# Short products as plain fp32 matmuls in a convolution and two-attention kernel on one core

## The reference

```python
# block 1
perceived = conv3x3_depthwise(x, w_perc) + b_perc        # 3 results for each channel
hid = gelu(w_up1 @ perceived + b_up1)                    # 256 channels
h = x + w_up2 @ hid + b_up2
q, k, v = split(h @ w_qkv.T + b_qkv)
scores = stack([(q * shifted(k, dy, dx)).sum(-1) for the 9 neighbours]) / sqrt(128)
h = h + sum(softmax(scores)[i] * shifted(v, i))
# block 2
xn = group_norm(h) * gamma + beta                        # 8 groups
q, k, v = xn @ Wq + bq, xn @ Wk + bk, xn @ Wv + bv
out = softmax(q @ k.T / sqrt(128)) @ v                   # 1024 x 1024
return xn + out @ Wp + bp
```

## Time and profile before

| | us |
|---|---|
| median of 3 runs | 1099.22 (1096.4 to 1099.63) |
| span of the profiled execution, first to last instruction | 1098.3 |
| PE busy | 1064.8 |
| PEld busy | 976.7 |
| DVE busy | 905.1 |
| ACT busy | 781.0 |
| POOL busy | 443.6 |

### The profile page before, as it was taken

One profiled execution on the slowest core, in us unless ns is written; L12 is line 12 of the kernel. 1 busy time (PEld: TensorE's weight loads), 2 busy tenths in 40 slices (PEclk: granted clock), 3 DMA queues, 4 the chain that ended last, 5 costly groups with the idle time before them and its releaser, 6 DMA issues.

```text
span 1098.3 us, 22684 instructions
## 1 busy us (share of the span) xinstructions
PE 1064.8 (97%) x7476; PEld 976.7 (89%) x7476; DVE 905.1 (82%) x1885; ACT 781.0 (71%) x1504; POOL 443.6 (40%) x399
## 2 busy tenths in 40 slices
PE   5988999999999999999999999999999999999997
PEld 5867989989899999999999999999999999998876
DVE  6957888788887888888788888878898888888874
ACT  2565686868677777767777776787777778677763
POOL 4634245361524527152452715335261533523130
PEclk9967999999999999999999999999999999999998
DMA  5101001020100102010010201001020100000000
GB/s 89 20 1 20 1 11 30 1 40 1 30 10 17 21 0 38 0 29 10 11 27 0 38 0 29 10 10 29 0 38 0 29 10 10 10 1 10 11 20 20
DMA packets 85496, 18.67 MB, mean 17 GB/s; under 512 B 67536, under 2 KB 85328, under 8 KB 85456
## 3 DMA queue, kind: packets, MB, share of 16 engines
q1 hardware_dynamic: 84608, 17.77, 8.7%
q10 hardware_dynamic: 848, 0.39, 0.2%
HBM read 9.76 MB, written 8.39 MB: 17 GB/s over the span
## 4 chain that ended last, share of the span: by engine, by line
PE 92%; DVE 4%; issue 2%; ACT 1%; POOL 1%; DMA 0%; ACTq 0%; DVEq 0%
PE work L476 20%; PE work L478 20%; PE work L477 20%; PE ps_t L636 10%; PE ps_s L476 5%; PE ps_s L477 5%; PE ps_s L478 5%; PE work L654 1%; PE work L562 1%; PE work L602 1%; PE work L571 1%; PE ps_t L664 1%; DVE et_lo L2006 1%; POOL g_lo L1519 1%; ACT et_hi L1104 0%
## 5 line engine op out<-in xcount | busy, mean ns | idle before, releaser
L1519 POOL TENSOR_TENSOR g_lo<-u,g_hi 128x512 fp32r<-128x512 f32 x60 | 78.2, 1304 | 349.4 <-ACT g_hi L1001 349.4
L1104 ACT ACTIVATE et_hi<-ps_t 128x1024 fp32r<-128x1024 f32 x128 | 131.1, 1024 | 66.4 <-PE ps_t L636 65.2
L2000 DVE TENSOR_REDUCE nm<-ps_s 128x1 f32<-128x1024 f32 x124 | 151.5, 1222 | 30.5 <-PE ps_s L478 28.9
L476 PE MATMUL work<-t_lo,wc_hi 128*128 128x256 f32 x576 | 166.8, 290 | 5.9 <-DVE wc_lo L1786 4.5
L2006 DVE TENSOR_TENSOR et_lo<-ps_t,et_hi 128x1024 fp32r<-128x1024 f32 x128 | 155.9, 1218 | 11.6 <-ACT et_hi L1104 8.9
L478 PE MATMUL work<-t_hi,wc_hi 128*128 128x256 f32 x576 | 162.7, 282 | 0.0
L477 PE MATMUL work<-t_hi,wc_lo 128*128 128x256 f32 x576 | 162.2, 282 | 0.0
L1094 ACT ACTIVATE e<-ps_s,nm 128x1024 f32<-128x1024 f32 x124 | 138.3, 1115 | 21.9 <-DVE nm L2000 19.8
L476 PE MATMUL work<-et_lo,vv_hi 128*128 128x256 f32 x512 | 147.5, 288 | 0.1
L478 PE MATMUL work<-et_hi,vv_hi 128*128 128x256 f32 x512 | 144.9, 283 | 0.0
L477 PE MATMUL work<-et_hi,vv_lo 128*128 128x256 f32 x512 | 144.5, 282 | 0.0
(11 more groups left out here) (213 smaller groups left out, 2965.0 us busy)
## 6 DMA issues: line engine op xcount, KB each, us to landing
x_in<-in_x SPq DMA_DIRECT2D x64, 128.0 KB, 3.4
out<-r_tok SPq DMA_DIRECT2D x32, 256.0 KB, 2.3
w_up_t<-in_L_conv_w_up SPq DMA_DIRECT2D x1, 384.0 KB, 4.3
y<-in_L_conv_w_qkv SPq DMA_DIRECT2D x1, 192.0 KB, 4.6
const<-in_const ACTq DMA_DIRECT2D x1, 166.0 KB, 5.6
y<-in_L_conv_w_up ACTq DMA_DIRECT2D x1, 128.0 KB, 5.5
const<-in_const ACTq DMA_DIRECT2D x1, 64.0 KB, 3.6
bv_row<-in_L_conv_b_qkv SPq DMA_DIRECT2D x1, 64.0 KB, 2.8
```

Of the source, the lines that this page charges most:

```text
L476: te.matmul(dst, wh, xl, start=first, stop=False)
L1104: act.activation(et_hi[:, :, (t % 4) * 128:(t % 4 + 1) * 128], ps_t[:, :].rearrange("p (k c) -> p k c", k=TILES), ACT.Copy) \
L1519: return pool.tensor_tensor(dst, full, hi, ALU.subtract)
L2000: dve.tensor_reduce(nm1[:, t:t + 1], score_tile(n, t)[:, :], AX.X, ALU.max, negate=True) \
```

## The change

Products with fewer than 256 moving columns lose their split operands: `v`, `local_scores`, `local_values` and `attended` become plain fp32 products. With that go `q_lo`, `kp_lo`, `v_hl`, `pt_lo`, `a_lo` and the instructions that made them, the matmul against zeros, and, because `attended` now takes the attended pixels as the stationary operand and so gives pixels on partitions, ACT's copy `a_t` and the transposes `final_t` as well. `v` reads `h` itself, so that it waits for `h_ready` and no longer for `h_lo_ready`. The transposed local weights get a buffer for each half image, and `halo_turn` writes straight into it. The bank of `pj` is now freed by DVE's `output`. All other calls keep their order on their engines.

```diff
-        kp_hi, kp_lo = (sb(f"kp_{p}", [128, HP, WP], F32R) for p in ("hi", "lo"))
-        v_full = sb("v_full", [128, 4, 128])
-        v_hl = sb("v_hl", [128, TILES, 2, 128], F32R)
+        q_c = sb("q_c", [128, PIX])
+        kp = sb("kp", [128, HP, WP])
+        v_pix = sb("v_pix", [128, TILES, 128])
...
-        pt_hi, pt_lo = (sb(f"pt_{p}", [128, 2 * W + 4 * WINDOW], F32R) for p in ("hi", "lo"))
+        pt_both = sb("pt", [128, 2, 2 * W + 4 * WINDOW])
+        pt = [pt_both[:, half] for half in range(2)]
...
-        FREED_BY = dict(conv=u_step, up2=h_ready, q=q_lo_ready, k=k_lo_ready, v=v_ready,
-                        at=pt_lo_ready, av=y_ready, gn=gn_step, qq=qq_lo_ready, kk=kk_lo_ready,
-                        vv=vv_lo_ready, pv=a_lo_ready, pj=a_t_ready, ft=o_ready, s0=e_ready, s1=e_ready)
+        FREED_BY = dict(conv=u_step, up2=h_ready, q=q_ready, k=k_ready, v=v_ready,
+                        at=pt_ready, av=y_ready, gn=gn_step, qq=qq_lo_ready, kk=kk_lo_ready,
+                        vv=vv_lo_ready, pv=a_ready, pj=o_ready, s0=e_ready, s1=e_ready)
...
             def v(n, half):
-                project_pixels("v", half, n, h_lo_ready, (w0_hi[:, 2], w0_lo[:, 2]), (h_hi, h_lo))
+                te.wait_ge(*h_ready.after(n, half))
+                te.wait_ge(*bank_free("v", half, n))
...
+                for t in range(4):
+                    pix = slice(half * HALF + t * 128, half * HALF + (t + 1) * 128)
+                    mm = te.matmul(bank("v", half, n)[:, t * 128:(t + 1) * 128], h[:, pix], wv0[:, :], start=True, stop=True)
+                mm.then_inc(pe["v"].handle, 1)
             def local_scores(n, j):
-                te.wait_ge(*q_lo_ready.after(n, j // 2))
-                te.wait_ge(*k_lo_ready.after(n, 1))
+                te.wait_ge(*q_ready.after(n, j // 2))
+                te.wait_ge(*k_ready.after(n, 1))
...
-                    qs = [x[:, t * 128:(t + 1) * 128] for x in (q_hi, q_lo)]
-                    ks = [x[:, 4 * t:4 * t + 6, :].rearrange("p r w -> p (r w)") for x in (kp_hi, kp_lo)]
-                    mm = mm3(dst, qs, ks)
+                    mm = te.matmul(dst, q_c[:, t * 128:(t + 1) * 128],
+                                   kp[:, 4 * t:4 * t + 6, :].rearrange("p r w -> p (r w)"), start=True, stop=True)
...
             def local_values(n, half):
-                te.wait_ge(*pt_lo_ready.after(n, 2 * half + 1))
-                te.wait_ge(*halo_lo_ready.after(n, half))
-                te.wait_ge(*v_lo_ready.after(n, 1))
+                te.wait_ge(*pt_ready.after(n, 2 * half + 1))
+                te.wait_ge(*halo_ready.after(n, 2 * half + 1))
+                te.wait_ge(*v_ready.after(n, 1))
...
-                te.matmul(dst[:, :].rearrange("p (r w) -> p r w", r=ROWS), w0_hi[:, 2],
-                          kp_hi[:, 0:1, 0:W].broadcast_to([128, ROWS, W]), start=True, stop=False)
                 for u in range(4):
                     t, before, behind = 4 * half + u, W if u else 0, W if u < 3 else 0
                     at = own_at(u)
-                    mm3(dst[:, u * 128 - before:(u + 1) * 128 + behind], (v_hl[:, t, 0, :], v_hl[:, t, 1, :]),
-                        [x[:, at - before:at + 128 + behind] for x in (pt_hi, pt_lo)], False, False)
+                    te.matmul(dst[:, u * 128 - before:(u + 1) * 128 + behind], v_pix[:, t, :],
+                              pt[half][:, at - before:at + 128 + behind], start=(u == 0), stop=False, skip_group_check=True)
...
             def attended(n, half):
-                te.wait_ge(*a_lo_ready.after(n, 2 * half + 1))
+                te.wait_ge(*a_ready.after(n, 2 * half + 1))
                 te.wait_ge(*bank_free("pj", half, n))
...
-                mm3(bank("pj", half, n)[:, :], (w1_hi[:, 2], w1_lo[:, 2]), (a_hi[:, :], a_lo[:, :])) \
-                    .then_inc(pe["pj"].handle, 1)
+                for t in range(4):
+                    pix = slice(t * 128, (t + 1) * 128)
+                    mm = te.matmul(bank("pj", half, n)[:, pix], a_c[:, pix], wv1[:, :], start=True, stop=True)
+                mm.then_inc(pe["pj"].handle, 1)
...
-            def final_t(n, half):
-                te.wait_ge(*a_t_ready.after(n, half))
-                te.wait_ge(*bank_free("ft", half, n))
-                for t in range(4):
-                    mm = te.transpose(bank("ft", half, n)[:, t * 128:(t + 1) * 128], a_t[:, t * 128:(t + 1) * 128], ident)
-                mm.then_inc(pe["ft"].handle, 1)
...
-            def halo_hi(n, half):
-                act.wait_ge(*halo_turned.after(n, 2 * half + 1))
-                act.wait_ge(*pe["av"].after(n, half - 1))
...
-            def v_lo_half(n, k):
-                pool.wait_ge(*v_hi_ready.after(n, k))
-                minus(v_hl[:, 4 * k:4 * k + 4, 1, :], v_full[:, :, :], v_hl[:, 4 * k:4 * k + 4, 0, :].bitcast(F32)) \
-                    .then_inc(v_lo_ready.handle, 1)
...
-                dve.wait_ge(*halo_lo_ready.after(n, j // 2 - 1))
-                dve.transpose(halo_t[0:W, two, :], pn[96:128, :, W + 128:WINDOW])
-                dve.transpose(halo_t[96:128, two, :], pn[0:W, :, 0:W]).then_inc(halo_turned.handle, 1)
...
+                dve.wait_ge(*pe["av"].after(n - 1, j // 2))
+                if is_first(n):
+                    dve.wait_ge(*cleared.after(0, 0))
+                dve.transpose(left_blocks(pt[j // 2])[:, two, :], pn[96:128, :, W + 128:WINDOW])
+                dve.transpose(right_blocks(pt[j // 2])[:, two, :], pn[0:W, :, 0:W]).then_inc(halo_ready.handle, 1)
...
-                dve.wait_ge(*pe["ft"].after(n, k))
+                dve.wait_ge(*pe["pj"].after(n, k))
```

More of the change, by code:

```diff
@@ L255, in conv_seq_kernel @@
         r_tok = sb("r_tok", [128, 4, 128])
-        a_at = region("a_mem", HALF)
-        a_hi, a_t = placed("a_hi", [128, HALF], a_at, F32R), placed("a_t", [128, HALF], a_at)
-        a_lo = sb("a_lo", [128, HALF], F32R)
+        a_c = sb("a_c", [128, HALF])
         bp_row = sb("bp_row", [128, 128])
@@ L575, in local_values @@
                     at = own_at(u)
-                    mm3(dst[:, u * 128 - before:(u + 1) * 128 + behind], (v_hl[:, t, 0, :], v_hl[:, t, 1, :]),
-                        [x[:, at - before:at + 128 + behind] for x in (pt_hi, pt_lo)], False, False)
+                    te.matmul(dst[:, u * 128 - before:(u + 1) * 128 + behind], v_pix[:, t, :],
+                              pt[half][:, at - before:at + 128 + behind], start=(u == 0), stop=False, skip_group_check=True)
                 t, rows, at = (4, 3 * 128 + 96, own_at(4) - W) if half == 0 else (3, 0, own_at(-1) + 128)
-                mm3(dst[:, rows:rows + W], (v_hl[:, t, 0, :], v_hl[:, t, 1, :]),
-                    [x[:, at:at + W] for x in (pt_hi, pt_lo)], False, True) \
-                    .then_inc(pe["av"].handle, 1)
+                te.matmul(dst[:, rows:rows + W], v_pix[:, t, :], pt[half][:, at:at + W],
+                          start=False, stop=True, skip_group_check=True).then_inc(pe["av"].handle, 1)
             def group_moments(n):
@@ L761, in fill_program @@
                 scores(0, 6)
-                final_t(0, 0)
                 probs_t(0, 5)
@@ L784, in fill_program @@
                 vv(1, 1)
-                final_t(0, 1)
             def turn_program(it):
@@ L826, in turn_program @@
                 v(c, 0)
-                final_t(a, 0)
                 scores(a, 7)
@@ L842, in turn_program @@
                 vv(b, 1)
-                final_t(a, 1)
             def drain_program():
@@ L880, in drain_program @@
                 k(B - 1, 0)
-                final_t(B - 3, 0)
                 up2(B - 1, 1)
@@ L911, in drain_program @@
                 probs_t(B - 2, 2)
-                final_t(B - 3, 1)
                 values(B - 2, 0)
@@ L926, in drain_program @@
                 group_moments(B - 1)
-                final_t(B - 2, 0)
                 values(B - 2, 2)
@@ L943, in drain_program @@
                 scores(B - 1, 3)
-                final_t(B - 2, 1)
                 vv(B - 1, 0)
@@ L958, in drain_program @@
                 probs_t(B - 1, 6)
-                final_t(B - 1, 0)
                 probs_t(B - 1, 7)
@@ L1014, in q_hi_half, with k_half @@
                     act.wait_ge(*scaled.after(0, 0))
[L1015 to L1018 removed]
+                act.activation(q_c[:, k * HALF:(k + 1) * HALF], bank("q", k, n)[:, :], ACT.Identity, bias=bq0_s) \
+                   .then_inc(q_ready.handle, 1)
+            def k_half(n, k):
                 act.wait_ge(*pe["k"].after(n, k))
@@ L1106, in et_hi_tile, with a_part @@
                    .then_inc(et_hi_ready.handle, 1)
-            def a_hi_part(n, j):
+            def a_part(n, j):
                 act.wait_ge(*pe["pv"].after(n, j))
-                act.wait_ge(*pe["ft"].after(n, j // 2 - 1))
-                act.activation(a_hi[:, (j % 2) * 256:(j % 2 + 1) * 256], bank("pv", j, n)[:, 0:256], ACT.Copy) \
-                   .then_inc(a_hi_ready.handle, 1)
-            def a_t_half(n, half):
```

(18 more changed lines are left out.)

349 lines of the change are left out of this document (94 added, 255 removed), and 20 rows, old and new, of tables (BANK_PLAN, DRAIN_PLAN, FILL_PLAN).

## The result

The changed kernel takes 1063.02 us, the median of 4 runs (1062.53 to 1063.94), against 1097.91 us for the kernel before in the same measurement: a ratio of 0.9682, with a 95% interval of 0.9668 to 0.9696. Forecast were 1060 us, in a range of 1042 to 1080. The profiled execution took 1062.82 us, its span is 1060.8.

The account below looks back on a forecast made before the run. PE, busy 97% of the span, was taken as the bound. Savings of 25.9 us in twelve turns, 7.7 filling and 5 draining sum to 38.6; 1098.3 less that, plus 0.9, gives 1060 us, range 1042 to 1080.

Parts of the forecast that it names:

- Price of a plain product: On PE, two records a product, each proportional to columns but at least 0.11 us: 0.22 at 128 columns, 0.34 at 204.
- Rival 1: On PE, columns don't matter below 256: all plain records at 0.11 us, giving 1036 us; chance 6%.
- rival 3: On PE, every quarter of a plain product pays a full matmul of 0.11 us: +3.5 us an image, 1155 us; chance 5%.
- Waits in the loop: New PE waits each turn: 0.10 us at up2(c, 0) for g_lo, 0.15 at values(a, 2) for output, 0.25 in all.
- Other engines' relief at nothing: Work taken off DVE, ACT and POOL costed at nothing, as they have 9 us and more of slack behind PE.
- Filling: Up to 212.78 us: 4.9 of PE products, 1.6 for the lower clock, 1.2 of the pt_lo wait; -7.7 us.
- the one at the lower clock: In the filling, 57 to 98 us, v of two halves and one local part cost twice as much: 1.6 us more saved.
- Draining: From 985.27 us on: 4.7 of PE products plus a shorter end, 6.0 us, of which 5 counted.
- this adds no new releaser: Bank of pj, freed by output instead of a_t's copy: output already freed the same banks for final_t; no wait added.
- The very end: Last chain, a_hi to output: a_lo, a_t and transposes leave, the product grows by 0.11; together some 1.7 us less.
- From span to time: Added 0.9 us, between the span of 1098.3 and the median of the runs, to 1059.7, giving 1060.6.
- Rival 2: Freed PE time turns into waits in the loop: a turn loses 1.2 us instead of 0.25, 1072 us; chance 19%.

Follow-up runs that it names:

- spare DVE work: Changed kernel plus DVE subtractions that nobody reads, of widths 170, 224 and 416, in the filling and draining alone: 1067.08 us.
- spare work only in the turns: Changed kernel plus DVE subtractions that nobody reads, of widths 170, 224 and 416, in the loop turns alone: 1064.92 us.
- spare work everywhere: Changed kernel plus a DVE subtraction that nobody reads at each place where DVE made a lo half: 1078.56 us.
- drain banks: Changed kernel with four DRAIN_PLAN entries altered, so values(14,0) no longer waits for output: 1058.59 us; with the loop's two waits also removed, 1053.72 us.

## Why the prediction was right, and where it was not

**Price of a plain product: right.** Proportional to the columns with a floor: 0.22 for 128 columns was forecast, 0.81/4 to 0.89/4 = 0.20 to 0.22 measured; a call of local_scores 0.68 forecast and 0.54 + 0.13 measured; a half of local_values 1.40 forecast, 1.33 and 0.08 in the call ahead measured. Rival 1 (width makes no difference, 0.44 a call of local_scores) and rival 3 (0.88 a call) fall with these rows. The rule of the Trainium skill (FP8 and Floating Point Precision, TensorE Precision Notes: four passes for true FP32) agrees: 204 columns in 0.34 us are 2.4 columns a nanosecond if each goes through four times, at a granted clock of 1.00. Passes are paid by columns here, so a narrow product does not pay four floors. Of local_values and attended the prediction read one half and doubled it, 1.82 and 0.77; the other halves take 1.91 (585.63 to 587.54) and 0.69 in the kernel before, which happens to cancel.

**Waits in the loop: right places, size 0.41 instead of 0.25.** 0.13 at up2 and 0.20 at values show in the two calls themselves; the run without them is 0.41 a turn shorter. Its turn of 61.82 also shows what PE saves without waits, 64.37 - 61.82 = 2.55 where 2.41 was forecast. So twelve turns came within 0.2 us because two misses, 1.7 us more saved and 1.9 us more waited, nearly cancel.

**Other engines' relief at nothing: right for the load in the loop, not for the chains and not for the ends.** The slack was there: DVE's old load put back costs a turn 0.12. But slack in busy time says nothing of a split that PE is waiting for: without the end of a_lo, 0.38 of v's 0.89 would have gone into a wait. The prediction did not see that the parts cover each other's chains, and its sum for PE holds because the same change happens to remove a_lo. At the ends the load put back costs some 4 us.

**Filling: -7.7 forecast, -12.0 measured.** The mis-sized term is, as far as the runs tell, the one at the lower clock, 1.6. Between 57 and 98 us the granted clock rose from 0.63 to 0.92, that is from (1 - 0.63) x 2 x 41 = 30 us at the lower level to 7. The prediction doubled the saving of the products that fall there and left the stretch itself as long as it was. With spare DVE work the clock is 0.83 and 3.45 us are gone; with spare work only in the turns it was 0.96, 3 us fewer at the lower level, and image 2's mean came 1.45 us sooner. The group mean of image 0 tells where the miss lies (the kernel before, the changed one, and the changed one's PE from 57 to 98 us):

```profile
92.78 0.42 PE L588 MATMUL work<-moments,const 128*128 128x2 f32 x2
...
84.35 0.28 PE L572 MATMUL work<-moments,const 128*128 128x2 f32 x2
...
57.00:98.00 41.00, 30.77 (x143) 0.92 0.10 13
```

Up to there 8.4 us went, where the prediction's terms for this stretch are 1.34 for three halves of v, 0.72 for one local part, 1.6 for the lower clock and 1.2 for the wait, in sum 4.9; behind it 3.6 us went where 2.9 was forecast. So 3.6 of the 4.3 are missed in the stretch with the lower clock. How much of them is the clock, how much the splits' absence from the chains, and how much the choice of the execution that was profiled before, is not separated.

**Draining: -5 forecast, +0.2 measured.** The step that failed is "this adds no new releaser". It was read from the loop's plan, where attended and final_t of a half stood in the same bank; in DRAIN_PLAN attended(13,1) had bank 0 and final_t(13,1) bank 2, and the next user of bank 0 now waits for output instead of a_t. The swap of four banks gives back 4.0, 2.5 of it wait and 1.5 clock. The very end was right: from the last copy to the end it was 1098.3 - 1091.21 = 7.09 and is 5.54 now, 1.55 less where 1.7 was forecast.

The end of the changed kernel's timeline (ACT's last copy, DVE's last output; the span ends at 1060.8):

```profile
1055.26 0.38 ACT L1065 ACTIVATE a_c<-work 128x256 f32<-128x256 f32 x1 [2.46 <-PE work L470]
...
1056.94 1.13 DVE L1887 SCALAR_TENSOR_TENSOR r_tok<-work,rec,r_tok 128x128 f32<-128x128 f32 x4 [5.01 <-PE work L596]
```

**From span to time: 0.9 added.** This compares one execution with the median of three, and it is not what lies around a span, which is 1.7 to 2.2 us in every run (1062.82 - 1060.8 = 2.0). It did little harm, since that execution lies 2.3 us above the median of four: from there the sum leads to 1097.9 - 38.6 = 1059.3.

**Rival 2** (a turn loses 1.2 us to waits) did not come: 0.41.

## What to carry to other kernels

Price a plain fp32 product by records: its columns, with a floor, times two, and compare with three split records at the floor; here 128 columns won clearly and 204 did not on PE. When an intermediate product goes, check who frees its bank in every hand-written plan, the first and last images too, not in the loop alone. And cut a PE stage together with the chain that it had covered: nearly half of v's gain came only with attended's.

## What the runs showed of the hardware that was not expected

- A DVE operation on two SBUF operands was held up beside one of POOL. In the kernel with spare work everywhere, two spare subtractions of 256 columns begin beside POOL's g_lo and take 1.87 us together; a third with POOL idle takes 0.42. The timeline of DVE and POOL:

```profile
632.91 0.42 DVE L1899 TENSOR_TENSOR spare_t<-spare_s 128x256 f32<-128x256 f32 x1
...
636.15 1.29 POOL L1440 TENSOR_TENSOR g_lo<-u,g_hi 128x512 fp32r<-128x512 f32 x1 [20.07 <-ACT g_hi L970]
...
636.18 1.87 DVE L1899 TENSOR_TENSOR spare_t<-spare_s 128x256 f32<-128x256 f32 x2
...
637.70 1.50 POOL L1440 TENSOR_TENSOR g_lo<-u,g_hi 128x512 fp32r<-128x512 f32 x1 [0.26 <-ACT g_hi L970]
```

  The pair ends at 638.05, 0.61 behind the end of g_lo at 637.44. The Trainium skill (SBUF — State Buffer, SBUF: two separate sides) says that DVE with two SBUF inputs and a GpSimd operation that reads SBUF lock a shared port pair, and that the later one waits for the whole instruction; this agrees. The next g_lo in turn took 1.50 in place of 1.29. Most of the removed splits read PSUM and one SBUF operand, and a_lo kept its 0.415 in the mean; only the halo's low half, 1.1 of the 7.4 us, read two from SBUF. So the runs with spare work bear harder on POOL's splits than the kernel before did, and what they cost is an upper estimate of the relief from DVE's load.
- A single wait of 3.8 us on PE was followed by a lower clock, 0.74 to 0.77 in the mean over the 7 us from 983 on, where the draining without that wait stayed at 1.00: a wait cost its own length and then some. Seven profiles have this wait, of 3.8 to 4.1 us, with a mean granted clock of 0.83 to 0.91 in the 20 us around it; the two kernels with drain banks wait 1.3 us at that place, and the clock around it is 1.00.
- Part of a call's time shows in the next call: behind the plain products of local_scores the same conv took 2.28 in place of 2.14 us, so distances between starts have to be read over the pair.
